# A decoder on one core: the output projection of the latent attention moved into the steps of its quads and of the cross attention's keys and values

## The chip, the cores and the metric

One Trainium2 chip, of which the kernel uses one core. The metric is the device time of one execution in microseconds (us). Engines are named as in the profile: PE is TensorE (PEld its weight loads), DVE VectorE, ACT ScalarE, POOL GpSimd; SP issues all DMAs, in one queue.

## What is computed

A decoder of two layers over x of 16 batches of 100 tokens, width 512, all in float32. The change concerns the first of its sublayers and the preparation of the second:

```python
# layer 0, latent attention (16 heads; each token's heads attend to each other)
scores = jnp.einsum('bsid,bsjd->bsij', q, k) * SCALER
attn = jax.nn.softmax(scores, axis=-1)
out = jnp.einsum('bsij,bsjd->bsid', attn, v).reshape(b, s, DKQV)
x = _layernorm(x + (out @ Wo + bo), axis=-1)
# layer 0, cross attention: keys and values of the context (16 x 361 x 512), 4 heads of 128
k = _rmsnorm((ctx @ Wk + bk).reshape(b, se, NKV, HD), kn_w)
v = (ctx @ Wv + bv).reshape(b, se, NKV, HD)
```

Then follow the cross attention itself, a sign-quantised feed forward, a causal attention, a memory attention and a quantised feed forward. The blocks of 64 of that last one's weights are quantised by a search over 16 scales, whose trials are spread over earlier stages.

## The kernel before

The program is a list of stages (`phases`, L3184). At the end of each, every engine waits until the stage's stores to DRAM have landed; SP also loads the next stage's first weights early (`load_next`). Every float32 product is made of three matmuls of high and low parts (`mm3`, L166): a high copy is made on ACT (`copy_hi`), the low rest on DVE (`sub_lo`).

`mla_project` (stage m1) writes queries, keys and values of the latent attention to the DRAM tensor `qkv`.

`kv_and_attend` (L1006, stage kv) interleaves three works in steps s = 0 to 50, each engine's instructions written out by hand in one Python loop per engine:
- 50 *quads* of 512 rows (a token's head is a row). Quad s: four transposes of its queries and keys (`turn_qk`, a step ahead), copies (`copy_q` on DVE, `copy_k` on ACT), scores of 4 x 128x128 (`score`), the negated maximum and its scaling on DVE (L1348, L1351), exponentials on ACT (L1269); in the next step the transposes of the probabilities (`turn_e`), their copy (L1254), the product with the values (`attend`), the division (L1344), and one step later the store to the DRAM tensor `attn` (L1102).
- 48 *context tiles*, three for each batch (128, 128 and 105 rows): transposes (`turn_ctx`, a step ahead), the projections to keys and to values (`project`, 12 matmuls of 512 columns each), the keys' bias add on DVE (L1337), their norm by ACT, DVE and POOL, and their transposes (`turn_k`, two steps behind).
- the quantiser's six chunks: POOL makes most trials (`pool_trial`), DVE some, ACT squares, DVE sums (L903).

Tile s and quad s share step s. As there are 50 quads and 48 tiles, steps 48 to 50 hold quads alone. The stage's ring of row tiles has LR = 6 members. PE uses all eight banks of PSUM, one for each of: context, turned keys, keys, values, rows, scores, turned probabilities, attended rows.

`mla_out` (L742, stage m3) follows: it splits Wo into high and low, then four groups of four batches: load of `attn` rows and of x, 16 transposes, copies, 48 matmuls that give the *transposed* product (128x400: stationary Wo, moving 400 tokens), bias on DVE (L466), 16 transposes back (`tail_pe`), the add of x, layer norm, and the store to `xs[1]`. Its loop is one of registers (`Fori`). Then `cross_attention` (stage ga) loads `xs[1]` in batches of 100 rows (L1504).

Of the kernel before, what the change touches and what calls it, by code (L numbers as in the profile page):

```python
# [29 lines left out]
ALU = mybir.AluOpType  # L30
# [78 lines left out]
def decoder(nc, t, out, stages=6):  # L109
# [632 lines left out]
    def mla_out():  # L742

        ph, ctx, G = "m3", ExitStack(), 4
        wo = [sb(f"{ph}_wo{s}", [P, KC, 512], F32R, ctx) for s in "hl"]
        w = weights( [
            (t["L0_attn_Wo"].rearrange("(k p) n -> p k n", p=P), 2048,
             [tuple(a[:].rearrange("p a b -> p (a b)") for a in wo)])])
        small, small_load, small_wait = small_loads(ph, ctx, [("bo", [P, KC], F32, column(t["L0_attn_bo"], KC))])
        keys = [("x", k) for k in range(KC)] + [("y", f) for f in range(KC)]  # L750
        g = Group(ph, ctx, G, attn, x0, xs[1], True, keys, bank[0:4])

        def do_sp():
            w["rest"]()
            small_load()
            g.stream()

        def do_pe():
            w["turn"]()
            w["ready"]()  # L760
            g.start_pe()
            with pe.Fori(0, g.iters) as i:
                g.turn_x(i)
                g.x_ready(i)
                g.project_out(i, wo, (g.xh, g.xl), KC)
                g.tail_pe(i)

        def do_act():
            w["hi"]()
            with act.Fori(0, g.iters) as i:  # L770
                g.x_hi(i)

        def do_dve():
            w["lo"]()
            small_wait(dve)
            def body(i):
                g.y_out(i, bias=small["bo"])
                g.normalise(i)

            g.dve_loop(body)  # L780

        def do_pool():
            with pool.Fori(0, g.iters) as i:
                g.rstd_pool(i)

        finish(ph, dict(early=w["first"], sp=do_sp, pe=do_pe, act=do_act, dve=do_dve, pool=do_pool), [g.stored()])
        ctx.close()


# [216 lines left out]
    def kv_and_attend():  # L1006
# [4 lines left out]

        ph, ctx = "kv", ExitStack()
# [5 lines left out]
        NT = max(NS, NQ) + 3  # L1018
        LR, OR = 6, 4
# [8 lines left out]
                     for c, w_ in (("k", wk), ("v", wv))])  # L1028
        small, small_load, small_wait = small_loads(ph, ctx, [
            ("bk", [P, W], F32, row(t["L0_xattn_bk"], P)),  # L1030
# [15 lines left out]
        O = [sb(f"{ph}_o{n}", [P, QU, DH], F32, ctx) for n in range(OR)]  # L1046
        NC = NKV_CHUNKS
# [17 lines left out]
                              "attended", "recip", "divided"))  # L1065
        rows = lambda s: KEYS[steps[s][1]]

        def do_sp():
# [9 lines left out]
            load_ctx(0)  # L1078
            load_ctx(1)
            load_rows(0)  # L1080
            w["rest"]()
            small_load()
            load_rows(1)
            load_ctx(2)
            load_ctx(3)
            for n in range(2, LR):
                load_rows(n)
            qz.start_sp()
            qz.load(1)
            for s in range(NT):  # L1090
                if s + 4 < NS:
                    since(sp, turned_c, s)
                    load_ctx(s + 4)
# [3 lines left out]
                if s == NS - 4:  # L1097
# [5 lines left out]
                if 1 <= s <= NS and steps[s - 1][1] == 2:  # L1103
                    j = steps[s - 1][0]
                    since(sp, v_made, s - 1)
# [3 lines left out]
                if 2 <= s <= NS + 1 and steps[s - 2][1] == 2:  # L1109
                    j = steps[s - 2][0]  # L1110
                    since(sp, k_lo, s - 2)
# [9 lines left out]
        def do_pe():  # L1121
# [60 lines left out]
            turn_ctx(0)  # L1182
            turn_qk(0)
            w["ready"]()
            for s in range(NT):
                if 1 <= s <= NQ:
                    turn_e(s - 1)
                if s + 1 < NS:
                    turn_ctx(s + 1)
                if s + 1 < NQ:  # L1190
                    turn_qk(s + 1)
                if s < NS:
                    since(pe, c_lo, s)
                    since(pe, k_made, s - 1)
                    project(s, wk, k_bank, k_full)
# [4 lines left out]
                if 2 <= s < NS + 2:  # L1200
                    turn_k(s - 2)
                if s < NS:
                    since(pe, v_made, s - 1)
                    project(s, wv, v_bank, v_full)

        def do_act():
# [39 lines left out]
            ctx_hi(0)  # L1246
            copy_k(0)
            for s in range(NT):
                if 1 <= s <= NS:
                    v_copy(s - 1)  # L1250
# [4 lines left out]
                if s + 1 < NS:  # L1255
                    ctx_hi(s + 1)
                if s + 1 < NQ:
                    copy_k(s + 1)
                squares(2 * s)
                if s < NS:  # L1260
                    kk = rows(s)
                    since(act, k_made, s)
                    since(act, k_sum, s - 2)
                    nc.scalar.activation(ksq[s % 2][0:kk, :], kraw[s % 4][0:kk, :], ACT.Square).then_inc(k_sq.sem, 1)
# [7 lines left out]
                if 2 <= s < NS + 2:  # L1272
                    key_hi(s - 2)
                squares(2 * s + 1)

        def do_dve():
# [43 lines left out]
            ctx_lo(0)  # L1320
            copy_q(0)
            qz.start_dve()
            for s in range(NT):
                b_ = s % 2
                if s + 1 < NQ:
                    copy_q(s + 1)
                if s + 1 < NS:
                    ctx_lo(s + 1)
# [4 lines left out]
                if s < NS:  # L1333
                    kk = rows(s)
                    since(dve, k_full, s)
                    since(dve, k_turned, s - 4)
                    nc.vector.tensor_tensor(kraw[s % 4][0:kk, :], k_bank[0:kk, :], small["bk"][0:kk, :], ALU.add)\  # L1337
# [14 lines left out]
                if s < NS:  # L1352
                    since(dve, k_sq, s)
                    since(dve, k_mean, s - 2)
                    nc.vector.tensor_reduce(kss[b_][0:kk, :], ksq[b_][0:kk, :].rearrange("p (h d) -> p h d", h=NKV),
                                            AX, ALU.add).then_inc(k_sum.sem, 1)
                    since(dve, k_sum, s)
                    since(dve, k_pow, s - 2)
                    nc.vector.tensor_scalar(kms[b_][:], kss[b_][:], 1.0 / HD, RMS_EPS, ALU.mult, ALU.add)\  # L1359
                        .then_inc(k_mean.sem, 1)  # L1360
                quant(2 * s + 1)
                if 2 <= s < NS + 2:
                    key_lo(s - 2)

        def do_pool():
            for s in range(NT):
                if s < NS:
                    kk, k_ = rows(s), kraw[s % 4]
                    since(pool, k_mean, s)
                    since(pool, k_norm, s - 2)  # L1370
# [1886 lines left out]
```

## Time and profile before

| | |
|---|---|
| median of three runs | 3165.73 us (3162.03 to 3168.84) |
| the profiled execution | 3160.35 us |
| its span in the profile | 3158.5 us |
| stage kv: first load, last store issued | 162.0, 644.9 us |
| stage m3: first load, last store issued | 647.0, 754.4 us |
| stage ga: first load issued | 760.5 us |
| busy share of the span: PE, PEld, DVE, ACT, POOL | 88, 79, 65, 53, 55% |
| mean granted clock of PE | 0.941 of 2.4 GHz |

A busy share is a mean over stages with different limits. The clock has two levels, 1.0 (2.4 GHz) and 0.5 (1.2 GHz); a stretch in between shows a mean. The time of a group of pipelined matmuls is read from start to start, since their durations overlap.

### The profile page before, as it was taken

What the parts mean: (1) busy time and instruction counts of PE and PEld (TensorE: products, weight loads), DVE (VectorE), ACT (ScalarE), POOL (GpSimd) and SP (SyncE); (2) the same over time, 40 slices, a digit from 0 to 9 for tenths busy, and PEclk for the clock granted to TensorE, in tenths of its full rate; (3) what the DMA queues carried; (4) which work ended last, traced back from release to release, by engine and by line L of the source; (5) the groups of instructions that cost most, each with busy time, mean ns of one, the idle gap of its engine ahead of it and who ended that gap; (6) DMA issues with size and microseconds to landing.
All of it is one profiled execution on the core that took longest, in us unless ns stands there. A gap on an engine that the chain in (4) does not pass through costs nothing. (4 is left out here: it accounts for less than half of the span.)

```text
span 3158.5 us, 48987 instructions
## 1 busy us (share of the span) xinstructions
PE 2777.5 (88%) x16162; PEld 2495.8 (79%) x16162; DVE 2065.2 (65%) x4090; ACT 1676.1 (53%) x4247; POOL 1727.2 (55%) x2145
## 2 busy tenths in 40 slices
PE   5789999964899999998599789999999997789998
PEld 4668888754788888886499778898888886669998
DVE  3467777743687888888446547677777777774334
ACT  1056666611788888776164355666656553443222
POOL 0057777700666766666154357888888786450000
PEclk9989999966999999998799889999999998889999
DMA  3545545434343333333321221321212111542101
GB/s 122 187 132 162 154 146 160 140 96 142 106 133 101 112 114 98 106 101 105 85 82 59 81 100 54 100 79 35 89 42 86 36 51 51 173 131 92 32 27 32
DMA packets 215374, 310.74 MB, mean 98 GB/s; under 512 B 47259, under 2 KB 112895, under 8 KB 213023
## 3 DMA queue, kind: packets, MB, share of 16 engines
q1 hardware_dynamic: 215134, 307.73, 31.1%
q8 instruction: 128, 2.10, 0.3%
q14 instruction: 112, 0.91, 0.1%
HBM read 211.30 MB, written 96.37 MB: 97 GB/s over the span
## 5 line engine op out<-in xcount | busy, mean ns | idle before, releaser
L925 POOL TENSOR_TENSOR mh_quant_d<-mh_quant_a,mh_quant_d 128x512 f32<-128x512 f32 x208 | 277.9, 1336 | 17.4
L1000 ACT ACTIVATE mh_quant_d<-mh_quant_d 128x512 f32<-128x512 f32 x256 | 159.8, 624 | 109.7 <-POOL mh_quant_d L925 109.4
L919 POOL TENSOR_SCALAR mh_quant_d<-mh_quant_a 128x512 f32<-128x512 f32 x208 | 132.9, 639 | 129.1 <-DVE mh_quant_err L903 81.3
L903 DVE TENSOR_REDUCE mh_quant_err<-mh_quant_d 128x8 f32<-128x512 f32 x256 | 173.6, 678 | 39.0 <-ACT mh_quant_d L1000 37.2
L1645 PE MATMUL bank<-ga_eT,ga_v 128*128 128x400 f32 (+1 forms) x384 | 169.9, 524 | 30.4 <-DVE ga_zl L1831 30.3
L1602 PE MATMUL bank<-ga_xt,ga_wqh 128*128 128x400 f32 x512 | 177.9, 410 | 1.6 <-DVE ga_xt L164 1.6
L2342 POOL TENSOR_TENSOR fq_var<-fq_mv,eps_ln 100x1 f32<-100x1 f32 x16 | 3.7, 229 | 315.5 <-DVE fq_mv L2285 315.5
L1371 POOL TENSOR_TENSOR kv_krs<-kv_kms,minus_half 128x4 f32<-128x4 f32 x48 | 50.0, 1042 | 230.0 <-DVE kv_kms L1359 228.7
L1795 ACT ACTIVATE ga_e<-ga_e,ga_nm 100x361 f32<-100x361 f32 x256 | 152.7, 597 | 38.5 <-DVE ga_nm L1890 37.0
L958 POOL TENSOR_TENSOR ga_quant_d<-ga_quant_a,ga_quant_near 128x512 f32<-128x512 f32 x128 | 165.2, 1291 | 13.5 <-DVE ga_quant_err L903 3.0
L1791 ACT ACTIVATE ga_e<-ga_e,ga_rs 100x361 f32<-100x361 f32 x256 | 152.6, 596 | 17.9 <-DVE ga_rs L1872 17.9
L1884 DVE SCALAR_TENSOR_TENSOR ga_e<-bank,ga_qrs,ga_mask 100x361 f32<-100x361 f32 x256 | 151.1, 590 | 14.3 <-PE bank L170 13.1
L1918 POOL TENSOR_TENSOR ga_qrs<-ga_qms,minus_half 100x4 f32<-100x4 f32 x64 | 68.3, 1068 | 168.3 <-DVE ga_qms L1825 168.3
L1774 ACT ACTIVATE ga_eT<-bank 128x300 f32<-128x300 f32 x256 | 106.4, 416 | 79.0 <-PE bank L1635 78.0
L923 POOL TENSOR_SCALAR mh_quant_d<-mh_quant_d 128x512 f32<-128x512 f32 x208 | 136.9, 658 | 17.2
L921 POOL TENSOR_SCALAR mh_quant_d<-mh_quant_d 128x512 f32<-128x512 f32 x208 | 132.9, 639 | 17.2
L1890 DVE TENSOR_REDUCE ga_nm<-ga_e 100x1 f32<-100x361 f32 x256 | 135.5, 529 | 6.7
L2731 ACT ACTIVATE mh_e<-mh_e,mh_nm 100x100 f32<-100x100 f32 x256 | 93.7, 367 | 86.2 <-DVE mh_nm L2846 86.2
L2302 DVE TENSOR_TENSOR fq_v<-fq_v 128x400 f32<-128x400 f32 x64 | 36.8, 575 | 136.6 <-ACT fq_v L2223 136.6
L1602 PEld LDWEIGHTS bank<-ga_xt,ga_wqh 128*128 128x128 f32 x512 | 97.4, 195 | 28.2 <-issue 2.0
L2223 ACT ACTIVATE fq_v<-bank 128x400 f32<-128x400 f32 x64 | 32.3, 505 | 163.8 <-PE bank L170 163.8
L168 PE MATMUL bank<-mh_zh,mh_woh 128*128 128x400 f32 x256 | 94.7, 370 | 25.6 <-DVE mh_acc L2805 16.5
(442 smaller groups left out, 10467.6 us busy)
## 6 DMA issues: line engine op xcount, KB each, us to landing
keys_turned<-kv_kt SPq DMA_DIRECT2D x16, 1448.0 KB
ga_kt<-keys_turned SPq DMA_DIRECT2D x64, 362.0 KB, 2.9
ga_xt<-x_turned SPq DMA_DIRECT2D x48, 400.0 KB, 4.9
mh_xt<-x_turned SPq DMA_DIRECT2D x48, 400.0 KB, 4.7
qkv<-m_rows SPq DMA_DIRECT2D x16, 1000.0 KB
kv_rows<-qkv SPq DMA_DIRECT2D x50, 320.0 KB, 3.3
raw<-x SPq DMA_DIRECT2D x64, 200.0 KB
kv_ctx<-in_ctx SPq DMA_DIRECT2D x32, 256.0 KB
```

The lines of the kernel that those rows point to most:

```text
L903: nc.vector.tensor_reduce(self.of(self.err, i)[:, s, :], self.error(i, s), AX, ALU.add).then_inc(self.summed.sem, 1)
L919: nc.gpsimd.tensor_scalar(e, a[:], 1.0 / SHRINKS[s], MAGIC, ALU.mult, ALU.add).then_inc(made.sem, 1)
L923: nc.gpsimd.tensor_scalar(e, e, -MAGIC, SHRINKS[s], ALU.add, ALU.mult).then_inc(made.sem, 1)
L925: nc.gpsimd.tensor_tensor(e, a[:], e, ALU.subtract).then_inc(self.diff.sem, 1)
L958: nc.gpsimd.tensor_tensor(self.d[s % 2][:], a[:], near[:], ALU.subtract).then_inc(self.diff.sem, 1)
L1000: nc.scalar.activation(self.error(i, s), self.error(i, s), ACT.Square).then_inc(self.squared.sem, 1)
L1602: last = nc.tensor.matmul(ps, wq[c // 2][:, k, w_], xt[:, k, c % 2, :], start=n == 0, stop=n == 11, skip_group_check=True)
L1645: last = nc.tensor.matmul(z_bank[:, 0:N], v[m % 3][0:kk, c, :], eT[m % 2][0:kk, c, :], start=c == 0, stop=c == 2, skip_group_check=True)
L1791: nc.scalar.activation(E[o % 4][:, 0:S2], E[o % 4][:, 0:S2], ACT.Copy, scale=rs[o % 4][:])\
L1795: nc.scalar.activation(E[n % 4][:, 0:S2], E[n % 4][:, 0:S2], ACT.Exp, bias=nm[n % 4][:], accum_out=sm[n % 4][:]).then_inc(exped.sem, 1)
L1884: nc.vector.scalar_tensor_tensor(out=E[n % 4][:, 0:S2], in0=score_bank[n % 2][0:S, 0:S2], scalar=qrs[g % 2][:, hh, j:j + 1], in1=small["ma ...
L1890: nc.vector.tensor_reduce(nm[n % 4][:], E[n % 4][:, 0:S2], AX, ALU.max, negate=True).then_inc(maxed.sem, 1)
```

## The change

`mla_out` is gone. Its work is done batch by batch inside `kv_and_attend`, as rows: attended rows are the stationary operand and Wo, 512 columns, the moving one, so the product comes out with tokens as rows, and no transposes back are needed. A batch's rows are complete with quad `last_quad[b]`; its projection stands four steps later, in steps 7, 10, 13 ... 50 and 53 (`out_at`). Context tile c now stands in step s = c + 3 (`SH`), so the first three steps hold quads alone. The transposes use the context's bank, the projection the keys' bank. The ring of row tiles shrinks to five. Wo is loaded in step 1 and split in step 4. All engines' orders are changed; SP's start too: five loads of rows, then the bias vectors, context tiles and x, then the quantiser's table.

```diff
-    phases = [mla_project, kv_and_attend, mla_out, cross_attention,
+    phases = [mla_project, kv_and_attend, cross_attention,
...
-        NT = max(NS, NQ) + 3
-        LR, OR = 6, 4
+        SH = 3
+        LR, OR, XR = 5, 4, 3
+        last_quad = [-(-S * H * (b_ + 1) // (P * QU)) - 1 for b_ in range(B)]
+        out_at = {n + 4: b_ for b_, n in enumerate(last_quad)}
+        NT = max(out_at) + 4
...
+                if s + 1 in out_at:
+                    b_ = out_at[s + 1]
+                    for n in range(last_quad[b_] - 3, last_quad[b_] + 1):
+                        since(sp, o_out[n % OR], n // OR)
+                    since(sp, turned_a, b_ - 1)
+                    sp.dma_start(at[:], rows_of(attn, b_)).then_inc(at_in.sem, 16)
...
+                if s - 3 in out_at:
+                    b_ = out_at[s - 3]
+                    since(sp, normed, b_)
+                    sp.dma_start(rows_of(xs[1], b_), x[b_ % XR][:]).then_inc(x_out[b_ % XR].sem, 16)
...
+            def turn_attended(b_):
+                since(pe, at_in, b_)
+                since(pe, c_lo, min(NS - 1, last_quad[b_] + 5 - SH))
+                for k in range(KC):
+                    last = nc.tensor.transpose(ctx_bank[:, k * S:(k + 1) * S], at[:, k * P:(k + 1) * P], ident[0:S, 0:S])
+                last.then_inc(turned_a.sem, 1)
+
+            def project_out(b_):
+                since(pe, a_lo, b_)
+                since(pe, k_made, min(NS - 1, last_quad[b_] + 4 - SH))
+                for k in range(KC):
+                    last = mm3(k_bank[0:S, :], ah[:, k, :], al[:, k, :], wo[0][:, k, :], wo[1][:, k, :], k == 0, k == KC - 1)
+                last.then_inc(a_full.sem, 1)
...
+                if 0 <= c < NS:
+                    since(pe, c_lo, c)
+                    since(pe, k_made, c - 1)
+                    if s - 1 in out_at:
+                        since(pe, added, out_at[s - 1])
+                    project(c, wk, k_bank, k_full)
                 if 1 <= s <= NQ:
                     attend(s - 1)
+                if s in out_at:
+                    turn_attended(out_at[s])
                 if s < NQ:
                     score(s)
...
+                if s in out_at:
+                    if out_at[s] == 0:
+                        w_out["ready"]()
+                    project_out(out_at[s])
...
+            def add_x(b_):
+                r = x[b_ % XR][:]
+                since(dve, a_full, b_)
+                since(dve, biased, b_)
+                nc.vector.tensor_tensor(r, k_bank[0:S, :], r, ALU.add).then_inc(added.sem, 1)
```

On DVE `attended_lo` stands in step s of `out_at` behind the maximum, `add_x` at the head of the next step, `variance` (statistics) in it behind the reciprocal, `normalise` at the end of the step after that. POOL adds the bias to x in step s and makes the reciprocal root of the variance at the head of step s + 2.

On PE, the stretch of a step before, from the end of the keys' projection to the next step (names: `kv_rows` a quad's rows, `kv_kraw` keys, `kv_ch`, `kv_cl` context high and low, `kv_w..` weights, `kv_e` probabilities; the last three rows of a projection stand for its twelve):

```order
L1178 MATMUL bank<-kv_rows,kv_eT 128x32 x4
L1163 MATMUL bank<-kv_kT,kv_qT 128x128 x4
L1145 MATMUL bank<-ident,kv_kraw 128x105 x4
L168 MATMUL bank<-kv_wvh,kv_ch 128x512
L169 MATMUL bank<-kv_wvl,kv_ch 128x512
L170 MATMUL bank<-kv_wvh,kv_cl 128x512
...
L1171 MATMUL bank<-ident,kv_e 128x128 x4
```

and the same stretch now, in step 7, the first of `out_at` (`kv_at` attended rows, `kv_ah`, `kv_al` their high and low parts, `kv_woh`, `kv_wol` the output weights):

```order
L1167 MATMUL bank<-kv_rows,kv_eT 128x32 x4
L1175 MATMUL bank<-ident,kv_at 128x100 x4
L1152 MATMUL bank<-kv_kT,kv_qT 128x128 x4
L1134 MATMUL bank<-ident,kv_kraw 128x105 x4
L168 MATMUL bank<-kv_wvh,kv_ch 128x512
...
L170 MATMUL bank<-kv_wvh,kv_cl 128x512
L168 MATMUL bank<-kv_woh,kv_ah 100x512
L169 MATMUL bank<-kv_wol,kv_ah 100x512
L170 MATMUL bank<-kv_woh,kv_al 100x512
...
L1160 MATMUL bank<-ident,kv_e 128x128 x4
```

Four transposes came ahead of the scores, and twelve matmuls between the values' projection and the next step's transposes of probabilities.

In SP's queue, the start of the stage before, and now:

```order
L1073 DMA kv_ctx<-in_ctx 128x512 x2
L1076 DMA kv_rows<-qkv 128x4x160
...
L571 DMA kv_kn<-in_L_xattn_kn_w 128x1
L1076 DMA kv_rows<-qkv 128x4x160
L1073 DMA kv_ctx<-in_ctx 105x512
L1073 DMA kv_ctx<-in_ctx 128x512
L1076 DMA kv_rows<-qkv 128x4x160 x4
L848 DMA kv_quant_tab<-in_shrinks 128x32
```

```order
L1048 DMA kv_rows<-qkv 128x4x160 x5
L571 DMA kv_bo<-in_L_attn_bo 100x512
L571 DMA kv_bk<-in_L_xattn_bk 128x512
...
L571 DMA kv_kn<-in_L_xattn_kn_w 128x1
L1045 DMA kv_ctx<-in_ctx 128x512 x2
L1045 DMA kv_ctx<-in_ctx 105x512
L1045 DMA kv_ctx<-in_ctx 128x512
L1051 DMA kv_x<-in_x 100x512 x3
L800 DMA kv_quant_tab<-in_shrinks 128x32
```

The rows moved ahead of the context tiles, one of them left the start, and a bias and three tiles of x came in ahead of the quantiser's table.

On DVE, the step behind step 7 now, from its head to the maximum (`kv_x` is x plus bias, then the sum):

```order
L1350 TENSOR_TENSOR kv_x<-bank,kv_x 100x512
L1327 COPY kv_qT<-bank 56x512
L164 TENSOR_TENSOR kv_cl<-bank,kv_ch 128x512
L855 TENSOR_REDUCE kv_quant_err<-kv_quant_d 128x8
...
L1378 RECIPROCAL kv_rs<-kv_sm 128x4
L1354 BN_STATS kv_stats<-kv_x 100x6
L1356 BN_AGGR kv_mv<-kv_stats 100x2
L1385 TENSOR_TENSOR kv_kraw<-bank,kv_bk 105x512
L1392 TENSOR_TENSOR kv_o<-bank,kv_rs 128x128
L1396 TENSOR_REDUCE kv_mx<-bank 128x4
```

The add of x is new ahead of the copy of queries, the statistics ahead of the keys' bias add.

## Rows read from the trace of the kernel before

**Rows 1.** Windows: us, busy us of PE PEld DVE ACT POOL, PEclk, DMA share, GB/s.
```profile
165.00:185.00 20.00, 13.84 (x65) 10.83 (x64) 11.48 (x19) 7.35 (x18) 2.93 (x3) 0.75 0.65 186
...
500.00:600.00 100.00, 99.99 (x598) 83.89 (x596) 80.64 (x158) 62.11 (x172) 78.60 (x91) 1.00 0.55 169
...
630.00:642.00 12.00, 8.53 (x36) 6.97 (x34) 4.95 (x13) 4.34 (x14) 0.69 (x1) 0.50 0.18 70
```

**Rows 2.** Timeline of PE over one full step (start, duration; a new group of four or twelve).
```profile
464.15 0.60 PE L1171 MATMUL bank<-ident,kv_e 128*128 128x128 f32 x4
464.59 0.52 PE L1129 MATMUL bank<-ident,kv_ctx 105*128 105x105 f32 x4
464.95 0.60 PE L1154 MATMUL bank<-ident,kv_rows 128*120 128x128 f32 x4
465.31 0.48 PE L168 MATMUL bank<-kv_wkh,kv_ch 128*128 128x512 f32 x1
...
468.19 0.97 PE L1178 MATMUL bank<-kv_rows,kv_eT 128*128 128x32 f32 x8
469.10 1.16 PE L1163 MATMUL bank<-kv_kT,kv_qT 56*128 56x128 f32 x8
470.18 0.58 PE L1145 MATMUL bank<-ident,kv_kraw 105*128 105x105 f32 x4
470.54 0.48 PE L168 MATMUL bank<-kv_wvh,kv_ch 128*128 128x512 f32 x1
...
473.43 0.60 PE L1171 MATMUL bank<-ident,kv_e 128*128 128x128 f32 x4
```

**Rows 3.** Timeline of PE's weight loads, the first of steps 48, 49 and 50.
```profile
622.93 0.59 PEld L1171 LDWEIGHTS bank<-ident,kv_e 128*128 128x128 f32 x4
...
629.56 0.71 PEld L1171 LDWEIGHTS bank<-ident,kv_e 128*128 128x128 f32 x4 [2.48 <-ACT kv_e L1269]
...
637.82 0.71 PEld L1171 LDWEIGHTS bank<-ident,kv_e 128*128 128x128 f32 x4 [1.97 <-ACT kv_e L1269]
```

**Rows 4.** Timeline of the stage's start, DVE and PE.
```profile
177.17 0.68 DVE L1306 COPY kv_qT<-bank 56x512 f32<-56x512 f32 x1 [4.99 <-DMA kv_quant_tab<-in_shrinks]
...
182.61 0.66 PE L1171 MATMUL bank<-ident,kv_e 128*128 128x128 f32 x4 [1.28 <-ACT kv_e L1269]
```

**Rows 5.** Waits from 183 to 622 us (us in total, times, longest).
```profile
DVE kv_qT L1306 <- PE bank L1154: 24.3, 37, 2.0
...
PEld bank L1171 <- ACT kv_e L1269: 5.4, 15, 0.6
```

**Rows 6.** Timeline at the borders of the old stage, PE and SP's queue.
```profile
655.75 2.93 PE L427 MATMUL bank<-ident,m_x 100*128 100x100 f32 x16 [14.21 <-DMA m_x<-attn]
...
754.36 0.33 SPq L392 DMA_DIRECT2D x<-m_res  x1
760.54 0.70 SPq L1504 DMA_DIRECT2D ga_x<-x  x2
```

**Rows 7.** Groups of instructions of the old stage, 641 to 762 us.
```profile
L498 DVE TENSOR_TENSOR m_res<-bank,m_res 100x512 f32<-100x512 f32 x16 | 10.6, 689 | 16.8 <-DMA m_res<-in_x 13.6 <-PE bank L437 3.1
...
L531 POOL TENSOR_TENSOR m_rstd<-m_var,minus_half 100x4 f32<-100x4 f32 x4 | 4.0, 1011 | 0.3
L164 DVE TENSOR_TENSOR m_wol<-raw,m_woh 128x2048 fp32r<-128x2048 f32 x1 | 2.3, 2293 | 4.5 <-ACT m_woh L161 4.5
L161 ACT ACTIVATE m_woh<-raw 128x2048 fp32r<-128x2048 f32 x1 | 1.9, 1909 | 7.8 <-DMA w_fc_quantised<-kv_quant_w 7.8
```

**Rows 8.** DMA issues (KB each, median us to landing).
```profile
values<-kv_v SPq DMA_DIRECT2D x16, 512.0 KB, 4.2
...
attn<-kv_o SPq DMA_DIRECT2D x50, 64.0 KB, 3.2
```

**Rows 9.** Line L1351: min/median/max ns; then its group, busy us, mean ns.
```profile
L1351 DVE TENSOR_SCALAR kv_nm<-kv_mx x50: 170/172/1111, 180.8 to 636.0; 128x4 f32<-128x4 f32 x50
...
L1351 DVE TENSOR_SCALAR kv_nm<-kv_mx 128x4 f32<-128x4 f32 x50 | 19.5, 390 | 1.7
```

More of the change, by code:

```diff
@@ L739, in mla_project @@
         ctx.close()
[L742 to L787, printed above, removed]
     class Quantiser:
@@ L1028, in kv_and_attend @@
                      for c, w_ in (("k", wk), ("v", wv))])
+        wo = [sb(f"{ph}_wo{s}", [P, KC, D], F32R, ctx) for s in "hl"]
+        w_out = weights([(t["L0_attn_Wo"].rearrange("(k p) n -> p k n", p=P), 2048, [flat(wo)])])
         small, small_load, small_wait = small_loads(ph, ctx, [
+            ("bo", [S, D], F32, row(t["L0_attn_bo"], S)),
             ("bk", [P, W], F32, row(t["L0_xattn_bk"], P)),
@@ L1065, in kv_and_attend @@
                               "attended", "recip", "divided"))
+        at_in = Signal(f"{ph}_at_in", B, 16)
+        x_in, x_out = ([Signal(f"{ph}_{c}{n}", len(range(n, B, XR)), 16) for n in range(XR)] for c in ("x_in", "x_out"))
+        batch = lambda name: Signal(f"{ph}_{name}", B)
+        biased, turned_a, a_hi, a_lo, a_full, added, stats_made, mv_made, eps_added, rstd_made, normed = (
+            batch(n) for n in ("biased", "a_turned", "a_hi", "a_lo", "a_full", "added", "stats", "mv", "eps_added", "rstd",
+                               "normed"))
         rows = lambda s: KEYS[steps[s][1]]
+        rows_of = lambda a, b_: a.rearrange("(b t) d -> b t d", t=S)[b_, :, :]
         def do_sp():
@@ L1090, in do_sp @@
             for s in range(NT):
-                if s + 4 < NS:
-                    since(sp, turned_c, s)
-                    load_ctx(s + 4)
+                c = s - SH
+                if s == 1:
+                    w_out["first"]()
+                if 0 <= c and c + 4 < NS:
+                    since(sp, turned_c, c)
+                    load_ctx(c + 4)
                 if 1 <= s and s - 1 + LR < NQ:
@@ L1332, in do_dve @@
                     nc.vector.reciprocal(rs[1 - b_][:], sm[1 - b_][:]).then_inc(recip.sem, 1)
[L1333 to L1337, printed above, removed]
+                if s - 1 in out_at:
+                    variance(out_at[s - 1])
+                if 0 <= c < NS:
+                    kk = rows(c)
+                    since(dve, k_full, c)
+                    since(dve, k_turned, c - 4)
+                    nc.vector.tensor_tensor(kraw[c % 4][0:kk, :], k_bank[0:kk, :], small["bk"][0:kk, :], ALU.add)\
                         .then_inc(k_made.sem, 1)
@@ L1373, in do_pool @@
                     three = k_[0:kk, :].rearrange("p (h d) -> p h d", h=NKV)
-                    nc.gpsimd.tensor_tensor(three, three, krs[s % 2][0:kk, :].unsqueeze(2).broadcast_to([kk, NKV, HD]), ALU.mult)\
+                    nc.gpsimd.tensor_tensor(three, three, krs[c % 2][0:kk, :].unsqueeze(2).broadcast_to([kk, NKV, HD]), ALU.mult)\
                         .then_inc(k_norm.sem, 1)
+                if s in out_at:
+                    b_ = out_at[s]
+                    r = x[b_ % XR][:]
+                    since(pool, x_in[b_ % XR], b_ // XR)
+                    nc.gpsimd.tensor_tensor(r, r, small["bo"][:], ALU.add).then_inc(biased.sem, 1)
```

168 lines of the change are left out of this document (106 added, 62 removed).

## The prediction, on record before the changed kernel ran

> **What bounds the kernel now.** I read the table of windows first [rows 1]. Inside the stage of the keys, values and quads, TensorE (PE) is busy 99.99 of 100 us at granted clock 1.00, while VectorE (DVE) has 80.6, GpSimd (POOL) 78.6 and ScalarE (ACT) 62.1. So work that is put into this stage costs time if it is PE's, and is free if it is another engine's and fits into 20 to 40% of slack. The timeline of one step [rows 2] shows what a step of 9.28 us is made of: four transposes of probabilities 0.44, four of context 0.36, four of rows 0.36, twelve matmuls for the keys 2.88, attention 0.91, scores 1.08, four transposes of keys 0.36, twelve matmuls for the values 2.89. The starts of the steps [rows 3, 4] say the same: step 1 starts at 182.61, step 48 at 622.93, 440.3 us for 47 steps, 9.37 each. PE waited for the exponentials only 5.4 us in all of them [rows 5].
>
> After step 47 it is different [rows 1, 3]: steps 48 and 49 have quads alone and take 6.63 and 8.26 us. The clock has gone to 0.50 in the second, after PE idled 2.48 us for the exponentials. The stage of the output projection then starts with 14.2 us in which PE waits for its first rows, and the next stage's first load leaves at 760.54, 6.2 us after the last store was issued [rows 6]. From 622.93 to 760.54 are 137.6 us in which PE is far from full.
>
> **The sum.** The change lets that stretch go and pays in four places. I follow one time, that at which the cross attention's first load leaves (760.54 now). What comes after it is the same code with the same inputs, and I take it as unchanged.
>
> *The start, +32.2 us.* Context step c now runs in step c + 3, so step 4, not step 1, is the first with a whole projection behind it. Now step 1 starts at 182.61, since DVE's second copy of queries waited until 177.17 for the quantiser's small table, and the table was queued behind the first loads [rows 4]. The order shows one row load (0.33 MB) fewer ahead of the table, but three of x and a bias (0.2 MB each) more: 0.5 MB, 2.6 us at the 186 GB/s of that stretch [rows 1]. Step 0 then ends at about 185.2. Steps 1 and 2 have quads alone. Their nearest row is step 49, 8.26 us at half clock [rows 3]. That step has no transposes of rows, which cost up to 0.4 us here, and step 2 also turns a context tile, 0.9 us if [rows 2]'s 0.44 doubles: 8.7 and 9.6 us. Step 3 is a full step without transposes of keys, 9.0 us, but begins at half clock: its three groups of transposes then cost 2.5 instead of 1.2 us, and I add 1 us for the part of the first projection ahead of the clock's rise: 11.3 us. Step 4 starts at 185.2 + 8.7 + 9.6 + 11.3 = 214.8. Ends: with light steps of 6.63 us and a full clock in step 3, 22 us; with the table 5 us later still, 38.
>
> *The output weights inside step 4, +1.9 us.* ACT splits them in 1.91 us, and DVE then takes 2.29 [rows 7]. Both lie between this step's transposed copies and its bias add. DVE comes to its maximum about 3 us late, of which 1.1 lie in the slack ahead of the exponentials. Ends: 0 and 4.
>
> *The projection itself, +48.6 us.* For each batch the order has four transposes of 100x100 and twelve matmuls of 512 columns with 100 stationary columns. By [rows 2] the nearest prices at full clock are 0.36 for the transposes of 105 columns and 2.88 for the twelve matmuls: 3.24 us. In the stage before the moving operand had 400 columns, now 512, with as many matmuls, 192. Fifteen batches fall on steps that are full of PE work (out steps 7 to 50): 15 x 3.24 = 48.6. Nothing hides it, as PE has no gap. The sixteenth is in the tail. The other engines' part per batch: DVE has a low copy (0.6), the add 0.69 [rows 7], and statistics and scaling over the same 100x512, which I price as the add: 2.7 us in three steps, against 1.8 us of slack in each (19.4% of 9.37). POOL has the power 1.01 [rows 7], an epsilon and a bias add that I price as the power, some 2.3 us in three steps; ACT has one copy. Both fit, now that those three steps also have 3.24 us more of PE.
> The Trainium skill (TensorE: Matmul & The Clock Gate, back-to-back issue gap) gives about 131 ns per matmul for sustained weight-load and matmul pairs of 512 columns. By that page the twelve would take 1.6 us and the term would be about 29 us. The trace does not agree: the twelve take 2.88 us in both projections of the step.
>
> *One wait is added on PE.* In the step after, the keys' projection waits until DVE has added x to the bank that both use. DVE starts that add when the last of the twelve ends, some 0.2 us into the step, and takes 0.69; PE meanwhile has 0.44 + 0.36 + 0.36 us of transposes and comes to the wait at about 1.2 us. Hidden by 0.2 us; without that cover all transposes, projections and quads are queued behind it. DVE's statistics lie ahead of its bias add, where it waits for PE now, so the maximum comes late only in steps with quantiser work of its own. I take 0.2 us per batch, 3 us in all. Ends: 0, and 16 (1.05 per batch: the add and half the statistics uncovered).
>
> *The last steps, -1.8 us.* Step 50 has no scores (1.08) and steps 49 and 50 no transposes of rows (2 x 0.36).
>
> *The tail, +18 us.* From the end of the projection of batch 14 to the next stage. SP's load of the last attended rows is queued behind the wait for the last values and behind their stores, whose landing takes 4.2 us [rows 8]: landed at about +3. Transposes at half clock 0.8, the two copies 1.3, twelve matmuls at half clock 5.8, add 0.9 with its wait, statistics 0.9, POOL's two 1.3, scaling 0.6, store 3.5 (as the 3.2 us of the small stores [rows 8]): 18.1. Ends: 12 (full clock, no queue) and 25 (the 6.2 us of the old store, and the keys' store ahead).
>
> Together: 182.6 + 32.2 + 1.9 + 440.3 - 1.8 + 48.6 + 3 + 18 = 724.8, against 760.5 now: **35.7 us less**. The profiled execution took 3160.35 us (its span 3158.5), so it would be 3124.6. The runs shown have their median 5.4 us above that execution, at 3165.73; I take the difference to them: 3130.
>
> SP's other new waits cost nothing. The load of attended rows goes out a step ahead and waits for a store issued the step before; the stores of x wait for scaling that ended about half a step earlier; a ring of five row tiles still leads by more than three steps.
>
> **The rivals.**
> 1. *The start is cheaper.* Light steps at 6.63 us, or a clock that stays up. For it: step 48 took that. Against it: that step began at full clock and still had a full step's work under way; the one after it fell to 0.50 [rows 1, 3]. Gain 35.7 + 10 = 46, with a short tail 52: 3114.
> 2. *DVE and POOL hold each other up.* DVE's scaling of the maxima takes 0.17 us as a rule, but 1.11 at worst [rows 9]; mean 0.39 over 50. The change gives DVE five more operations per batch and POOL three. If each of the eight meets such a hold-up of the mean excess of 0.22 us and half are on the chain to the exponentials, it is 0.9 us per batch, 13 in 15 in place of the 3 taken, a gain of 26; with all of them on it 26 in place of 3, a gain of 13. In the middle: 3146. Against it, PE's longer out step hides those of one step in three.
>  The Trainium skill (SBUF, who interferes with whom) says that DVE in a two-port mode, or with two SBUF inputs against a POOL operation that reads SBUF, and POOL lock each other out for a whole operation. The trace bears out that something holds short DVE operations for up to one POOL operation; not that the new ones meet it.
> 3. *DVE becomes the bound of the step after: slower.* Its head now waits for the last of the twelve matmuls, and all its work of that step is behind it: 7.6 us as now (80.6% of 9.37) plus 1.5. If the chain to the exponentials were the whole of this, 0.2 + 9.1 + 1.6, that step would take 10.9, and 1.5 to 3 us more with a quantiser's own trial or preparation in it. Add a scaling that waits for POOL's power behind its trials (1.3): about 3.3 us per batch, 50 in 15, in place of the 3 taken: 47 more, 11 slower than before: 3177. It decides from 2.6 us per batch on, (35.7 + 3) / 15. Against it: before the copy of queries DVE waits for PE in 37 of 47 steps, 24.3 us in all [rows 5], and only what stands ahead of the maximum delays the exponentials.
> 4. *The tail or the start is clogged by transfers*, both upper ends at once, 5.8 and 7 us: a gain of 23, 3143.
>
> **How the numbers follow.** My forecast, a gain of 22 to 46 us, has 0.62; rival 1 beyond that 0.12, rival 2 0.11, rival 4 0.07. In 0.03 it comes to nothing, as several of these at once, and rival 3 has 0.05. A measurement of this kernel can tell 0.2%, 6.3 us, from no change. Only rival 3 is slower by more: 0.05. Within it: 0.03. Faster: 0.92. The range of 8 in 10 reaches from rival 1 to a part beyond rival 2: 3112 to 3156.
>
> **What the changed profile would show.** Right: starts of steps 1, 2 and 3 some 9 us apart at clock 0.50, step 4 near 215 us; between steps 5 and 50 PE still over 98% busy at clock 1.00, out steps of 12.5 us and others of 9.3; about 18 us from the last full projection to the first load of the cross attention at about 725. Wrong: PE waiting for the add of x ahead of the keys' projection, or for the exponentials more than 10 us in all, or out steps above 13 us; then the term of 3 us falls. If the cross attention takes more or less time than now (its first load to the end), the assumption that all behind is unchanged falls.

## The result, and the profile of the changed kernel

The changed kernel takes 3127.06 us (median of 4 runs, 3123.20 to 3133.36) against 3165.37 for the kernel before beside it (4 runs, 3162.03 to 3168.84): 0.9879 of it, with a 95% interval of 0.9859 to 0.9900. The forecast was 3130. The profiled execution took 3130.44 us with a span of 3127.9 and a mean granted clock of 0.944.

The sum in the prediction followed one time, the cross attention's first load. One line of the x tile's group gives it (minimum, median and maximum ns of the issue, then the first and last start):

```profile
L1572 SPq DMA_DIRECT2D ga_x<-x x16: 274/297/1481, 725.2 to 837.4; - x16
```

It now leaves at 725.2; the sum had 724.8, and it was 760.54 [rows 6]. PE's timeline of the quads' transposes gives the borders of steps 1 to 5 and of step 50:

```profile
183.26 1.12 PE L1160 MATMUL bank<-ident,kv_e 128*128 128x128 f32 x4 [7.29 <-ACT kv_e L1290]
...
191.51 1.12 PE L1160 MATMUL bank<-ident,kv_e 128*128 128x128 f32 x4 [2.53 <-ACT kv_e L1290]
...
200.41 1.12 PE L1160 MATMUL bank<-ident,kv_e 128*128 128x128 f32 x4 [2.52 <-ACT kv_e L1290]
...
212.04 0.60 PE L1160 MATMUL bank<-ident,kv_e 128*128 128x128 f32 x4
...
222.52 0.66 PE L1160 MATMUL bank<-ident,kv_e 128*128 128x128 f32 x4 [1.37 <-ACT kv_e L1290]
...
696.80 0.60 PE L1160 MATMUL bank<-ident,kv_e 128*128 128x128 f32 x4
```

The first three take 1.12 us for four transposes: half clock (0.50, the 1.2 GHz level) with PE idle for the exponentials ahead of each. From step 4 they take 0.60, full clock (0.66 in step 5, where PE waited 1.37 us first). The windows say the same, and show where full PE ends to be full (columns as in [rows 1]):

```profile
165.00:185.00 20.00, 5.93 (x24) 4.75 (x24) 8.04 (x12) 3.95 (x12) 1.64 (x3) 0.50 0.84 241
500.00:600.00 100.00, 98.28 (x580) 81.36 (x579) 77.81 (x153) 54.31 (x149) 73.80 (x87) 1.00 0.50 152
630.00:642.00 12.00, 12.00 (x73) 9.79 (x73) 9.78 (x20) 7.69 (x23) 11.01 (x16) 1.00 0.76 238
```

The window of 630 to 642, half idle before [rows 1], is now full. But PE in 500 to 600 has fallen from 99.99 to 98.28. The waits from 183 to 690 us show what took it, over the whole stretch (us in total, times, longest):

```profile
PEld bank L1160 <- ACT kv_e L1290: 20.7, 14, 7.6
DVE kv_x L1350 <- POOL kv_x L1442: 17.9, 9, 3.4
PE bank L1160 <- ACT kv_e L1290: 15.4, 8, 7.3
...
PE bank L168 <- DVE kv_x L1350: 4.7, 5, 1.5
```

The two lines on the exponentials hold one long wait, of PE and of its weight loads, at the end of step 0 (7.3 and 7.6 us), where there was 1.28 [rows 4]. The second and the last line are new: DVE's add of x waits for POOL's add of the bias, and PE's projection of the keys waits for DVE. In one step, on POOL, DVE and PE:

```profile
548.24 1.39 POOL L1433 TENSOR_TENSOR kv_krs<-kv_kms,minus_half 128x4 f32<-128x4 f32 x1
549.71 1.04 POOL L1436 TENSOR_TENSOR kv_kraw<-kv_kraw,kv_krs 105x512 f32<-105x512 f32 x1
550.71 1.26 POOL L1442 TENSOR_TENSOR kv_x<-kv_x,kv_bo 100x512 f32<-100x512 f32 x1
...
552.07 0.69 DVE L1350 TENSOR_TENSOR kv_x<-bank,kv_x 100x512 f32<-100x512 f32 x1 [1.94 <-POOL kv_x L1442]
...
550.83 0.60 PE L1143 MATMUL bank<-ident,kv_rows 128*120 128x128 f32 x4
552.91 0.47 PE L168 MATMUL bank<-kv_wkh,kv_ch 128*128 128x512 f32 x1 [1.48 <-DVE kv_x L1350]
```

The projection's last matmul began at 549.72. DVE could have added then, but POOL had a trial of the quantiser, the power (L1433) and the scaling (L1436) ahead of the bias, and came to it at 550.71. That step took 11.1 us (549.96 to 561.07) in place of 9.3 to 9.4. Of the 14 steps behind an output, five take 10.5 to 11.1 and two more 9.7 and 9.8.

Behind 725.2 the changed kernel takes 2402.7 us to its end, the one before took 2398.0 from 760.54. The first use of each stage's x by PE splits it: cross attention 795.3 us (797.1 before), first feed-forward 255.9 (256.6), causal attention **898.5 (891.0)**, memory attention 133.5 (133.5). Two stages got shorter, 2.5 us together, and one 7.5 us longer. So 35.3 us were won where I looked, and the profiled spans show 30.6.

### The profile page after: what moved, and what is told of

It is laid out like the page before. It is cut to its first block and busy times, and to the rows that moved or that the text cites. A ratio compares the mean times of both kernels' runs of the same rounds, so it can differ in the third digit from the quotient of the medians.

```text
span 3127.9 us, 48858 instructions
## 1 busy us (share of the span) xinstructions
PE 2778.2 (89%) x16098; PEld 2484.4 (79%) x16098; DVE 2058.0 (66%) x4074; ACT 1676.9 (54%) x4247; POOL 1757.1 (56%) x2185
## 5 line engine op out<-in xcount | busy, mean ns | idle before, releaser
L1713 PE MATMUL bank<-ga_eT,ga_v 128*128 128x400 f32 (+1 forms) x384 | 169.9, 525 | 30.3 <-DVE ga_zl L1899 30.2
L871 POOL TENSOR_SCALAR kv_quant_d<-kv_quant_a 128x512 f32<-128x512 f32 x78 | 48.8, 626 | 225.2 <-DVE kv_quant_a L838 183.6
L1952 DVE SCALAR_TENSOR_TENSOR ga_e<-bank,ga_qrs,ga_mask 100x361 f32<-100x361 f32 x256 | 151.1, 590 | 13.9 <-PE bank L170 12.9
L1670 PEld LDWEIGHTS bank<-ga_xt,ga_wqh 128*128 128x128 f32 x512 | 96.8, 194 | 28.1 <-issue 2.0
L168 PE MATMUL bank<-mh_zh,mh_woh 128*128 128x400 f32 x256 | 94.6, 370 | 21.6 <-DVE mh_acc L2873 12.5
```

Of the source, the lines that this page charges most:

```text
L168: nc.tensor.matmul(ps, wh, xh, start=first, stop=False, skip_group_check=True)
L871: nc.gpsimd.tensor_scalar(e, a[:], 1.0 / SHRINKS[s], MAGIC, ALU.mult, ALU.add).then_inc(made.sem, 1)
L1670: last = nc.tensor.matmul(ps, wq[c // 2][:, k, w_], xt[:, k, c % 2, :], start=n == 0, stop=n == 11, skip_group_check=True)
L1713: last = nc.tensor.matmul(z_bank[:, 0:N], v[m % 3][0:kk, c, :], eT[m % 2][0:kk, c, :], start=c == 0, stop=c == 2, skip_group_check=True)
```

## The experiments

"First load" is the cross attention's; "5 to 50" is from the start of step 5 to that of step 50; "causal" is the length of the causal attention; "half" is the time in it at granted clock 0.50. The last four columns come from one profile each. Times are medians, and ratios are to the runs of the kernel before beside them (3165.37 for the changed kernel, then 3162.68, 3164.38 and 3163.80 in three further sets).

| kernel | us | 95% interval of the ratio | first load | 5 to 50 | causal | half |
|---|---|---|---|---|---|---|
| before | 3165.37 | | 760.5 | 418.1 | 891.0 | 92 |
| changed | 3127.06 | 0.9859 to 0.9900 | 725.2 | 474.3 | 898.5 | 113 |
| bias early | 3122.72 | 0.9851 to 0.9888 | 719.2 | 467.0 | 898.2 | 110 |
| no lead | 3127.06 | 0.9871 to 0.9901 | 724.3 | 469.8 | 899.8 | 108 |
| lead alone | 3169.75 | 1.0016 to 1.0040 | 770.8 | 422.5 | 890.1 | 91 |
| quarter projections | 3134.64 | 0.9891 to 0.9924 | 727.0 | 479.8 | 898.0 | 99 |
| quarter, bias early | 3097.75 | 0.9770 to 0.9828 | 693.6 | 446.3 | 892.9 | 94 |
| no lead, bias early | 3119.42 | 0.9843 to 0.9900 | 717.2 | 462.6 | 892.6 | 90 |
| bias and table early | 3113.30 | 0.9819 to 0.9880 | 709.6 | 466.9 | 892.8 | 94 |
| table early | 3120.26 | 0.9835 to 0.9878 | 718.7 | 474.3 | 899.4 | 107 |
| late | 3152.20 | 0.9954 to 0.9981 | 750.6 | 474.6 | 892.9 | 94 |
| changed, again | 3127.76 | 0.9866 to 0.9905 | 726.4 | 474.3 | 896.6 | 98 |

How far one profile can be trusted shows in six of them that share their program up to step 5 (changed, again, late, bias early and the two quarter runs): step 1 started between 182.76 and 185.92 us, step 5 between 221.58 and 223.72. A difference of one or two us at the first load is therefore nothing. The length of steps 5 to 50 is firmer: the four kernels with the same steps (changed, again, table early, late) took 474.3, 474.3, 474.3 and 474.6.

**Bias early.** Is POOL's queue the hold behind the outputs?

```
-                if s in out_at:
-                    b_ = out_at[s]
+                if s + 1 in out_at:
+                    b_ = out_at[s + 1]
                     r = x[b_ % XR][:]
                     since(pool, x_in[b_ % XR], b_ // XR)
```

> POOL adds the bias to x one step earlier. Theory A (the add of x waits for POOL's bias add, which is queued behind POOL's other work: 17.9 us of DVE's time and 4.7 us of PE's in the changed kernel): both waits go, the seven steps of 9.8 to 11.1 us behind an out step become 9.4 to 9.8, and the cross attention's first load leaves 4 to 8 us earlier than 725.2. Theory B (DVE and POOL hold each other's operations up, wherever they stand): those steps stay near 10.5 and the load moves by less than 2 us.

Steps 5 to 50 take 7.3 us less, and the long steps have gone to 9.3 to 9.6 but for one of 10.3. DVE's add no longer waits for POOL at all, only for PE, and PE is full again:

```profile
DVE kv_x L1350 <- PE bank L170: 19.1, 12, 2.5
...
500.00:600.00 100.00, 100.00 (x587) 83.06 (x587) 80.00 (x157) 58.90 (x162) 78.67 (x91) 1.00 0.52 156
```

The wait is POOL's place in the queue, not POOL's load: it does the same work here. The time itself gained 4.3 us between the medians, with intervals that overlap, and the first load 6.0, though step 1 started 2.7 us later in this profile; the 7.3 us in steps 5 to 50 is the firmer number.

**No lead**, and **lead alone.** The two parts of the change, each by itself. In the first the quads run in their old steps (SH = 3 becomes SH = 0, with turn_ctx(0), ctx_hi(0) and ctx_lo(0) ahead of the loops again), and the loads go out in the old order:

```
-        SH = 3
+        SH = 0
-            for n in range(LR):
-                load_rows(n)
+            load_ctx(0)
+            load_ctx(1)
+            load_rows(0)
+            small_load()
+            load_rows(1)
...
```

> The projection stays inside the steps, but context tile c stands in step c again (SH = 0), with the first loads in the order of the kernel before. Theory A (each of the three steps with quads alone costs 8 to 9 us at the start, and at the end of the stage only 6.6 and 8.3 us for two, plus about 11 us for the step that holds batch 14's projection): the first load of the cross attention at about 718, 7 us (2 to 12) earlier than 725.2. Theory B (running the quads ahead is what hides the start's weights and the last projections): 3 to 12 us later than 725.2.

In the second the quads lead and the old output stage stands:

```
+    def mla_out():
...
-        out_at = {n + 4: b_ for b_, n in enumerate(last_quad)}
-        NT = max(out_at) + 4
+        out_at = {}
+        NT = NQ + SH + 2
...
-    phases = [mla_project, kv_and_attend, cross_attention,
+    phases = [mla_project, kv_and_attend, mla_out, cross_attention,
```

> The kernel before with its own stage of the output projection, but with quads three steps ahead (context tile c in step c + 3, ring of five). Theory A: the start costs about 27 us, steps 48 to 50 give back 15: the old stage's first load leaves at about 659 instead of 647.4, and the kernel is some 12 us slower than before (ratio 1.004). Theory B (the shift is a gain by itself): the load at or ahead of 647, ratio 1.000 or below.

By itself the lead costs 7 us of time and 10.3 at the first load, where 12 was expected: it moves light steps from the end, where an idle stage border followed anyway, to a start at half clock. Steps 1 to 3 take 28.1 us there, steps 48 and 49 of the kernel before 14.9. With the projection inside the steps the lead is neutral, 0.9 us at the first load and the same median, and both theories of that run missed: I had expected 2 to 12 us earlier without it, or 3 to 12 later. So nearly all of the gain is that the old stage is gone and its matmuls stand among others.

**Quarter projections.** One of the four sets of three matmuls is issued; the other nine are left out, so the projection is computed in part only.

```
-                for k in range(KC):
-                    last = mm3(k_bank[0:S, :], ah[:, k, :], al[:, k, :], wo[0][:, k, :], wo[1][:, k, :], k == 0, k == KC - 1)
+                for k in range(1):
+                    last = mm3(k_bank[0:S, :], ah[:, k, :], al[:, k, :], wo[0][:, k, :], wo[1][:, k, :], True, True)
```

> The changed kernel with nine of the twelve matmuls of each batch's output projection left out (its output is another). Theory A (PE is the bound of the stage, 0.232 us a matmul): 15 x 9 x 0.232 = 31.3 us in the steps and some 3 in the tail, the cross attention's first load at about 691. Theory B (other engines or waits bound the out steps in part): less than 25 us, load after 700.

This was the instructive miss of theory A. Three quarters of the matmuls of a term that I had priced at 48.6 us were left out, and steps 5 to 50 grew by 5.5 us. Out steps fell to 10.3 to 10.9, but the steps behind them rose to as much as 14.7, and the waits name the chain:

```profile
PE bank L168 <- DVE kv_x L1350: 30.3, 14, 3.5
DVE kv_x L1350 <- POOL kv_x L1442: 24.8, 13, 3.4
```

The matmuls that I left out were the cover of POOL's queue. DVE's adds show it: that of step 35 comes 15.03 us after the start of the step in both kernels (537.04 to 552.07, and 540.08 to 555.11 here), though PE was done with the projection 2 us sooner here. In eleven of the fourteen out steps the two kernels agree in this within 0.04 us.

That explains why little is won, and not why the steps grew. The rest is the clock. PE now waits up to 3.48 us, and in each of the six longest steps behind an output, after its wait, stands a stretch of 3.4 us at granted clock 0.50, 20.5 us in all; the changed kernel has none between steps 5 and 50. PE in the quarter kernel, then the windows behind that wait here and behind the same wait of 1.48 us in the changed kernel:

```profile
555.95 0.47 PE L168 MATMUL bank<-kv_wkh,kv_ch 128*128 128x512 f32 x1 [3.48 <-DVE kv_x L1350]
```

```profile
557.00:560.40 3.40, 3.40 (x10) 2.62 (x9) 1.43 (x4) 0.00 (x0) 3.07 (x5) 0.50 0.00 0
```

```profile
553.95:557.35 3.40, 3.40 (x23) 2.99 (x22) 2.43 (x7) 0.63 (x1) 3.07 (x5) 1.00 0.02 5
```

By an estimate from these stretches (half of 20.5 us) the clock cost 10.2 us. Without it the steps would have been 4.7 us shorter than the changed kernel's, not 5.5 longer.

If POOL's queue is what sets these steps, both edits together must give what neither gave.

**Quarter, bias early.** The two diffs above in one kernel, with nine of twelve matmuls of each projection left out again.

> The changed kernel with nine of the twelve matmuls of each projection left out (three remain, so the projection is only a quarter computed) and with POOL's add of the bias issued one step earlier. Theory A (in the run with the quarter projections alone, POOL's add of the bias, queued behind the trials' work, took PE's place as what sets the step behind): with the add issued a step earlier the matmuls left out come through, out steps 10.1 to 10.4 us, steps behind them 9.3 to 9.5 instead of 11 to 14.7; first load of the cross attention near 690, 30 to 38 us before the quarter run's; time 3092 to 3102. Theory B (without PE's cover another engine, VectorE with its copies and trials, is next): steps behind an out step stay at 10.3 us or more, under 20 us come off, time 3112 to 3122.

The first load comes at 693.6, 33.4 us ahead of the quarter run's, and the time is 3097.75. Some 10 of these 33 us are the clock again: no stretch between steps 5 and 50 is at 0.50 here. Of the 30.2 us that the nine matmuls are worth in 14 out steps (14 x 9 x 0.24), 20.7 come through against the run with the early bias alone (467.0 to 446.3). Of the rest the waits show a part: seven of the steps behind an output take 10.0 to 12.2, and PE still waits 5.7 us for DVE's add, which itself waits for others only once in these steps, 0.4 us, so that what is ahead of it on DVE sets it. That work was not taken apart. So both theories hold in part; the time lies in the range of the first, the steps partly in that of the second.

**No lead, bias early.**

> No lead of the quads (and loads in the order of the kernel before), projection inside the steps, and the bias add a step earlier. Theory A (the lead of three steps brings nothing in itself, it only moves work from the end to the start): the bias add brings here what it brought with the lead, 4 to 6 us: time 3120 to 3124, within 2 us of the run with lead and early bias add. Theory B (the lead pays once POOL's hold is gone, since the output's steps then lie where no quad's work fills them): 3126 to 3130, 4 us or more over it.

The early bias brings 7.1 us at the first load here and 6.0 with the lead. Whether the quads lead or not makes no difference that the times can tell (3119.42 and 3122.72, overlapping intervals; 3.3 us apart where theory A had 2).

**Table early**, alone and with the bias early. Step 0 still waits for the quantiser's table, now for longer (7.3 us idle ahead of step 1, above), since SyncE issues it behind five loads of rows, four of context and three of x.

```
-            for n in range(LR):
+            load_rows(0)
+            small_load()
+            qz.start_sp()
+            load_rows(1)
+            qz.load(1)
+            for n in range(2, LR):
                 load_rows(n)
-            small_load()
...
-            qz.start_sp()
-            qz.load(1)
```

> The changed kernel with only the order of SyncE's first loads changed (rows 0, short vectors, table and first weights of the trials, then the rest); POOL's add of the bias stays where the change put it. Theory A (start and POOL's hold are separate costs that add): step 1 starts at 174 to 177 instead of 183.3, the steps behind the outputs keep their 10.5 to 11.1 us, the first load of the cross attention comes 7 to 10 us before the changed kernel's 725.2, time 3117 to 3120. Theory B (POOL's longer stretch for the trials takes the gain back): under 4 us at the first load, time 3123 to 3127.

> Bias add a step earlier, and SyncE issues the table of the trials and their first weights right behind the first rows and the short vectors, ahead of the other rows, the context and x. Theory A (step 0 is held by VectorE waiting for that table, the copies of step 0 queued behind it): step 1 starts at 176 to 180 instead of 185.9, time 4 to 7 us under the run with the bias add alone: 3116 to 3119. Theory B (the loads it passes are late instead, context of quads 0 to 3 for PE): step 1 starts no earlier than 184, time 3121 to 3125.

Step 1 starts at 176.8 and, with both, at 175.2, and all or nearly all of it arrives at the first load: 6.5 us alone (718.7; 7 to 10 were expected), 9.6 on top of the early bias (709.6). The second figure flatters the edit by the late start of the bias run's own profile (185.92); in time it is 9.4 us between the medians, more than the 4 to 7 expected. In PE's timeline of the kernel with both, ahead of step 1, the 7.29 us of idle time are 2.60:

```profile
175.21 1.12 PE L1162 MATMUL bank<-ident,kv_e 128*128 128x128 f32 x4 [2.60 <-ACT kv_e L1292]
```

This kernel, at 3113.30 us, is the fastest that computes everything, 14 us under the changed one and 51 under the one before.

**Late**, and **changed, again.** The causal attention's 7.5 us were left. Its program is unchanged, and PE waits for nothing ahead of its value matmuls, yet their mean has grown; the same group before and after (busy us, mean ns | idle):

```profile
L168 PE MATMUL bank<-mh_wvh,mh_xt 128*100 128x512 f32 x256 | 107.0, 418 | 0.1
```

```profile
L168 PE MATMUL bank<-mh_wvh,mh_xt 128*100 128x512 f32 x256 | 110.2, 430 | 0.1
```

Between groups of batches PE pauses for 2.55 us, near 181, 235 and 290 us into the stage in both kernels. Windows of 3 us around the pause near 181 us into the stage, in the kernel before:

```profile
1995.50:1998.50 3.00, 1.00 (x9) 0.83 (x7) 0.19 (x1) 1.90 (x5) 2.75 (x4) 1.00 0.00 0
1998.50:2001.50 3.00, 2.44 (x13) 1.90 (x14) 2.74 (x5) 1.61 (x4) 1.66 (x4) 1.00 0.28 87
2001.50:2004.50 3.00, 3.00 (x23) 2.73 (x22) 1.36 (x4) 1.55 (x3) 2.75 (x5) 1.00 0.36 94
2004.50:2007.50 3.00, 3.00 (x18) 3.00 (x18) 2.57 (x9) 2.84 (x12) 1.92 (x2) 1.00 0.00 1
```

and in the changed kernel:

```profile
1957.30:1960.30 3.00, 1.39 (x11) 1.22 (x9) 0.00 (x0) 1.52 (x4) 2.75 (x5) 1.00 0.00 0
1960.30:1963.30 3.00, 2.07 (x7) 1.77 (x8) 2.10 (x4) 1.98 (x5) 1.93 (x3) 0.51 0.26 87
1963.30:1966.30 3.00, 3.00 (x8) 1.98 (x7) 1.00 (x2) 0.00 (x0) 2.81 (x4) 0.50 0.28 88
1966.30:1969.30 3.00, 3.00 (x21) 2.63 (x20) 1.13 (x2) 1.55 (x3) 2.17 (x3) 0.85 0.00 0
```

PE is idle for the same 2.55 us, but then gets half clock for 6.8. The stretches behind the three pauses, 6.8, 6.8 and 3.4 us, make 17 us at half clock, 8.5 us of work lost; the kernel before has none there. Two runs ask whether the program or the moment decides. "Late" puts a chain of small transfers ahead of the cross attention, so that the causal attention starts near its old time; the other is the changed kernel itself once more.

```
...
+            for k in range(18):
+                sp.dma_start(pad_in[:], t["L0_attn_bo"].partition_broadcast(1)).then_inc(pad_sem, 16)
+                sp.wait_ge(pad_sem, 16 * (k + 1))
             load_x(0)
```

> The changed kernel with a chain of 18 small transfers, each waited for, ahead of the first load of the cross attention, so that all that follows starts some 36 us later and the causal attention starts near 1815 as in the kernel before (1817.5). Theory A (the 7.5 us that the causal attention is longer since the change are stretches of half clock behind pauses of PE of 2.5 us near 181, 235 and 290 us into the stage, which the clock answers or not according to when they fall): at the old start these stretches go, the stage takes 890 to 892 us, and the kernel is 28 to 30 us over the changed one, not 36. Theory B (something that the old output stage left behind in memory or semaphores): the stage still takes 898 to 900 us with the same half-clock stretches, and the kernel is 36 us over.

> The changed kernel itself, unaltered, profiled and timed a second time beside the others. Theory A (which pauses of PE the clock answers is a matter of when they fall, and can differ between executions of one kernel, as the four runs of the changed kernel with mean clocks of 0.944 and 0.949 and spans of 3128 to 3130 and 3121 to 3122 hint): the causal attention takes anything from 890 to 899 us, and its half-clock stretches beyond the first 80 us need not be the three of the first profile; the stages before it keep their 795 and 256 us. Theory B (the program sets them): 898 to 899 us again, with the same three stretches. Time 3122 to 3131 in both.

The 18 transfers took 25.5 us, not 36, so the stage began at 1807.5 and not at its old 1817.5. The kernel is 25 us over the changed one. The stage took 892.9 us, with no half-clock stretch between 100 and 370 us in; around the first pause:

```profile
1985.50:1988.50 3.00, 1.63 (x13) 1.46 (x11) 0.00 (x0) 1.27 (x3) 2.70 (x4) 1.00 0.00 0
1988.50:1991.50 3.00, 1.82 (x10) 1.48 (x11) 2.31 (x4) 2.24 (x5) 1.46 (x3) 1.00 0.22 62
1991.50:1994.50 3.00, 3.00 (x22) 2.53 (x22) 1.40 (x4) 1.35 (x3) 2.75 (x5) 1.00 0.39 113
```

The unaltered kernel, run again, had two stretches of 3.4 us in place of three of 17 in all, and 896.6 us. So the program doesn't set them. Its six runs point the same way without a trace, though not to a stage: spans from 3115.2 us at mean clock 0.951 to 3128.2 at 0.947.

## Why the prediction came out right, step by step

- *The start, +32.2.* Step 4 starts at 212.04, not at 214.8. DVE's copy behind the table came at 179.03, 1.9 us later than before where I had 2.6 (1.4 to 4.5 in the six profiles), but step 1 at 183.26 was only 0.7 later (185.2 was the sum; it lies within the six). The light steps took 8.25 and 8.90 against 8.7 and 9.6. Step 3 at 11.63 was the 11.3 of the sum, at a mean clock of 0.76: it began at half clock, as argued.
- *Output weights, +1.9.* Step 4 took 10.48 us, 1.1 over a full step.
- *Projection, 15 x 3.24.* Out steps take 12.4 to 12.5, but for one of 12.9, against 9.3 to 9.4: 3.1 each. The trace stands against the 131 ns per matmul that the Trainium skill (TensorE: Matmul & The Clock Gate, Back-to-back issue gap) gives for such pairs: the twelve of the changed kernel began 0.23 to 0.24 us apart too, but the first.
- *The added wait on PE, +3.* **This is the term that failed.** Steps 5 to 50 took 474.3 us; the sum had 469.4 (45 x 9.37, less 0.36, and 14 x 3.44; its 440.3 us for 47 steps run from a matmul to a weight load, from matmul to matmul they are 440.6, which leaves the 9.37). With the bias early they take 467.0, which is the sum without its wait (466.6). The wait costs 7.3 us, where I had 3, and by another way than I had priced: not DVE's own 0.69 us behind the matmuls, but POOL's bias add of 1.29 us (the median; 1.26 to 1.75), queued behind its power, scaling and trials, which DVE waits for. I had written that POOL's three operations "fit", because POOL has room on average. PE's wait for the add, which I had named as the sign against this term, makes 4.7 of the 7.3 us. The bound from above, 16, took it in. POOL's add takes 1.86 times DVE's of the same tile (1.286 against 0.692 us); the Trainium skill (GPSIMD Engine Reference, Elementwise — side-by-side cycle accounting) has 1.96 for an fp32 add of 2048 columns. By that page it would have been about 1.35 us, an estimate from DVE's 0.69, nearer than the 1.01 of the power that I used.
- *Last steps and tail, -1.8 and +18.* From the last full projection (ended 706.9) to the first load are 18.3 us.
- *What comes after is unchanged.* False by 4.7 us: the causal attention's 7.5, less 2.5 and 0.3 elsewhere. Of the 7.5 the three stretches at half clock would give all, but the length does not follow the clock alone (below). The three deviations of the sum, 3.6 us less up to step 5, 4.9 more in the steps, 0.9 less from step 50 on, all but cancel at the first load. The profiled execution came out 5.8 us over the sum's 3124.6, most of it these 4.7. The median is 3.4 below that execution, where I had put it 5.4 above, so part of the closeness of 3127 to 3130 is luck of two signs.
- *The rivals.* The start was cheaper by 3.6 us, not by 10 (2.4 to 4.5 in the six profiles). Rival 2 had DVE and POOL hold each other up and put it on the scale of the maxima; the hold-up came, at some half of that price, through a semaphore between them and not through a longer add: DVE's took 690 to 693 ns all sixteen times. Rival 4 did not happen. Rival 3 didn't happen, but the quarter run shows how near it stands: with less of PE's work, VectorE's head behind POOL, and the half clock behind PE's wait, set the step at up to 14.7 us.

## What to carry to other kernels

When work moves between engines' queues, list for each new semaphore what stands ahead of it in the queue of the engine that gives it: an engine with a fifth to a quarter of its time free can still answer 2 us late, and a step earlier in its program is often all the cure. Cutting the work of the bounding engine tests whether it bounds: here a quarter of the matmuls cost more time than all of them, until the queue behind them was put right. Such a cut also makes waits, and half clock can follow a wait, so the granted clock of both kernels belongs beside the result. And a stage that got longer without a change in its waits is to be read by its granted clock before anything else.

## What the runs showed of the hardware that was not expected

- **One pause, two clocks.** The same 2.5 us of idle PE are followed by full clock (2.4 GHz) in one execution and by 3.4 or 6.8 us at 1.2 GHz in another, of the same stage and even of the same kernel. Over twelve profiles the causal attention's length less half its time at half clock is 842 to 848 us, while the length itself runs from 890 to 900 with 90 to 113 us at half clock. The Trainium skill (TensorE: Matmul & The Clock Gate, The HAM clock gate) says of a kernel's start that the monitor runs freely and that the number of slow matmuls there varies from run to run with its phase. The two profiles of the changed kernel show the like in the middle of a stage (17 and 7 us at half clock behind the same three pauses). The half clock is not the whole of it: the quarter run's stage took 898.0 us with 99 us at half clock, "again" 896.6 with 98. What decides the clock in a given execution these runs don't show: the starts of 1765.0 and 1807.5 us gave the same pattern, that of 1770.4 another.
- **POOL's power on one column** took 0.56 us for 100 rows, against 1.01 to 1.39 for the four columns of 128 rows.
